# Two sorts of expert rows instead of three in a fused attention and mixture-of-experts block, and a weight ring of five places

## The reference, cut to what matters

```python
x = x + tanh(g_xattn[0]) * L0_xattn(layernorm(x), ctx)
x = x + tanh(g_ffn[0])   * L0_ffn(layernorm(x))      # 8 experts, top 2
x = x + tanh(g_xattn[1]) * L1_xattn(layernorm(x), ctx)
x = x + tanh(g_ffn[1])   * L1_ffn(layernorm(x))      # MLP 256-1024-1024-1024-256

# L0_ffn
probs = softmax(xf @ Wr);  topk_p, topk_i = top_k(probs, 2)
out = sum_k topk_p[k] * (xf @ Wi[topk_i[k]]) @ Wo[topk_i[k]]
# L1_ffn
h = silu(x @ w1 * s1) * (x @ w2 * s2)
h = gelu(h @ h1 * t1);  h = gelu(h @ h2 * t2);  return h @ w3 * s3
```

## Time and profile before

| | |
|---|---|
| median of 3 runs | 1046.01 us (1044.91 to 1046.17) |
| the profiled execution: time, span | 1046.19 us, 1044.4 us |
| granted TensorE clock, mean | 0.994 |
| busy: PE, DVE, ACT, POOL | 97%, 48%, 46%, 29% |
| sorted groups 2 and 4, period | 120.1 and 120.2 us |
| groups 1, 3, 5, 6, period | 91.7 to 91.8 us |

### The profile page before, as it was taken

One profiled execution on the slowest core, in us unless ns is written; L12 is line 12 of the kernel. 1 busy time (PEld: TensorE's weight loads), 2 busy tenths in 40 slices (PEclk: granted clock), 3 DMA queues, 4 the chain that ended last, 5 costly groups with the idle time before them and its releaser, 6 DMA issues.

```text
span 1044.4 us, 14384 instructions
## 1 busy us (share of the span) xinstructions
PE 1012.4 (97%) x5218; PEld 823.8 (79%) x5218; DVE 500.7 (48%) x1388; ACT 477.0 (46%) x877; POOL 303.4 (29%) x428
## 2 busy tenths in 40 slices
PE   7999999899999999999999999999999999999996
PEld 4778777678789877887898878778888788788885
DVE  5487768676343543463325434643245245134321
ACT  1355545446544545364344453644444435434431
POOL 0015653311710541216205423153044221112111
PEclk9999999999999999999999999999999999999999
DMA  9930015513475554344755553537545535344440
GB/s 340 378 121 1 2 61 168 187 52 102 141 259 182 178 155 151 115 146 132 251 177 157 178 155 98 160 121 252 187 152 191 161 102 180 103 135 147 141 141 23
DMA packets 44252, 158.85 MB, mean 152 GB/s; under 512 B 6443, under 2 KB 6827, under 8 KB 43282
## 3 DMA queue, kind: packets, MB, share of 16 engines
q0 software_dynamic: 29952, 104.88, 32.5%
q1 hardware_dynamic: 10826, 40.63, 11.4%
q10 hardware_dynamic: 3400, 12.38, 3.0%
HBM read 137.93 MB, written 29.36 MB: 160 GB/s over the span
## 4 chain that ended last, share of the span: by engine, by line
PE 83%; DVE 8%; ACT 4%; issue 2%; DMA 1%; POOL 1%; DVEq 0%; SPq 0%; POOLq 0%; ACTq 0%
PE psum L1027 56%; PE psum L921 2%; PE psum L1099 2%; PE psum L1101 2%; PE psum L1100 2%; PE psum L1075 1%; PE psum L820 1%; DVE x_residual L1882 1%; PE psum L830 1%; PE psum L678 1%; PE psum L947 1%; PE psum L702 1%; PE psum L716 1%; PE psum L929 1%; DVE ln_stats L1574 1%
## 5 line engine op out<-in xcount | busy, mean ns | idle before, releaser
L2258 POOL DMA_DIRECT2D mlp_pieces<-in_mlp x176 | 96.8, 557 | 424.2 <-PE psum L1027 420.7
L1027 PE MATMUL psum<-hidden_a_high,mlp_pieces 128*128 128x512 f32 x512 | 205.7, 402 | 0.0
L1027 PE MATMUL psum<-hidden_b_high,mlp_pieces 128*128 128x512 f32 x512 | 202.9, 396 | 0.0
L1027 PE MATMUL psum<-hidden_a_low,mlp_pieces 128*128 128x512 f32 x512 | 199.6, 390 | 0.0
L1027 PE MATMUL psum<-hidden_b_low,mlp_pieces 128*128 128x512 f32 x512 | 199.6, 390 | 0.0
L2105 DVE TENSOR_TENSOR hidden_a_low<-hidden_a,hidden_a_high 128x512 fp32r<-128x512 f32 x128 | 88.1, 688 | 174.2 <-ACT hidden_a_high L1497 173.4
L2105 DVE TENSOR_TENSOR hidden_b_low<-hidden_b,hidden_b_high 128x512 fp32r<-128x512 f32 x64 | 44.4, 693 | 169.6 <-ACT hidden_b_high L1497 169.6
L1027 PEld LDWEIGHTS psum<-hidden_a_high,mlp_pieces 128*128 128x128 f32 x512 | 96.1, 188 | 23.6 <-issue 2.8
L1514 ACT ACTIVATE hidden_a<-psum,mlp_scales 128x512 f32<-128x512 f32 x64 | 44.1, 689 | 154.4 <-PE psum L1027 154.4
L1027 PEld LDWEIGHTS psum<-hidden_a_low,mlp_pieces 128*128 128x128 f32 x512 | 96.2, 188 | 21.7 <-issue 2.6
L1027 PEld LDWEIGHTS psum<-hidden_b_high,mlp_pieces 128*128 128x128 f32 x512 | 96.2, 188 | 20.2 <-issue 0.8
(11 more groups left out here) (283 smaller groups left out, 1809.6 us busy)
## 6 DMA issues: line engine op xcount, KB each, us to landing
mlp_pieces<-in_mlp POOLq DMA_DIRECT2D x176, 512.0 KB, 4.0
slots<-in_zeros SPq DMA_DIRECT2D x3, 3072.0 KB, 36.6
yrows<-expert_rows ACTq DMA_DIRECT2D x18, 512.0 KB, 3.0
mlp_piece_to_examine<-in_mlp SPq DMA_DIRECT2D x16, 512.0 KB, 4.0
slot_rows<-slots SPq DMA_DIRECT2D x15, 512.0 KB, 4.5
x_residual<-in_x SPq DMA_DIRECT2D x4, 1024.0 KB, 24.2
out<-x_residual SPq DMA_DIRECT2D x8, 512.0 KB, 3.4
expert_in<-in_Wi SPq DMA_DIRECT2D x1, 2048.0 KB, 15.7
```

The costliest lines, as they stand in the source:

```text
L1027: last = mm(o, a, b, start=(k == 0 and i == 0), stop=(k == n_k - 1 and i == len(parts) - 1))
L2258: pool.dma_start(mlp_ring[:, r % RING, :], d["mlp"][r % NCHECK]).then_inc(ring_in[r % RING], 16)
```

## The change

Batches 2 and 3 are sorted together. `SORTS` has two entries, batch 1 alone and batches 2 and 3: 23 and 39 slot tiles (2 x 16 + 7), 62 in place of 69, in 12 and 20 pairs. Batch 1 stays where it was. The double sort is routed in group 1 (`ranked_in`), its expert products stand in group 2 (`routed_in`), and group 4 has neither. `xm` holds one batch, so the second batch is normalised over the first after the transposes of the first; its rows are scattered in group 1, and batch 2's rows are normalised once more in group 2 (`r_norm_again`) and scattered there. The ring has five places, which makes room for routing buffers of 16 tiles.

```diff
-RING = 6
+RING = 5
-NSB = B - 1
-EB = 23
+SORTS = [(1, 1), (2, 2)]
+EB = [2 * n + E - 1 for n in NJ]
...
+        def ranked_in(n):
+            return n if n < NS else None
+        def turns_at(s, w12, c):
+            if s == 0:
+                return c - 1 if w12 and 1 <= c <= 4 else None
+            return (c - 1 if 1 <= c <= 4 else None) if w12 else (c + 4 if c < 4 else None)
+        def logits_at(s, w12, c):
+            if s == 0:
+                return c - 2 if w12 and 2 <= c <= 5 else None
+            return (c - 2 if 2 <= c <= 5 else None) if w12 else (c + 3 if 1 <= c < 5 else None)
+        def steps_of(s):
+            if s == 0:
+                return {"copy": -2, "max": -1, "exp": 0, "mask": 0, "rank": 1, "coef": 1, "slots": 1, "tiles": 3}
+            return {"copy": 4, "max": 5, "exp": 5, "mask": 6, "rank": 6, "coef": 7, "slots": 7, "tiles": 10}
+        def pairs_at(s, c):
+            if s == 0:
+                return {3: (0, 1), 4: (2, 3, 4), 5: (5, 6), 6: (7, 8, 9), 7: (10, 11)}.get(c, ())
+            return {1: (0, 1, 2), 2: (3, 4, 5), 3: (6, 7, 8), 4: (9, 10, 11), 5: (12, 13, 14), 6: (15, 16, 17),
+                    7: (18, 19)}.get(c, ())
...
 PE, r_turn:
+                    bank = 6 + p % 2 if p < 4 else 4 + p % 2
+                    pe.wait_ge(xm_r, 2 * (R0[s] + p) + 2)
 PE, group, after the product of t:
+                            if r is not None and layer == 0 and turns_at(r, False, c) is not None:
+                                r_turn(r, turns_at(r, False, c))
+                            if r is not None and layer == 0 and logits_at(r, False, c) is not None:
+                                r_logits(r, logits_at(r, False, c))
+                            if r is not None and t == steps_of(r)["rank"]:
+                                r_rank(r)
 ACT, group, after gelu and high of t:
+                            if r is not None and layer == 0 and turns_at(r, False, c) is not None:
+                                r_turn(r, turns_at(r, False, c))
+                            if r is not None and HC * layer + c == steps_of(r)["exp"]:
+                                r_exp(r)
 DVE:
+            def r_norm_again(s):
+                dve.wait_ge(sc_done[s], 16 * 2 * JT)
+                for j in range(JT):
+                    normalise(JT + TJ[s] + j, xm[:, j, :], xa_r)
 DVE, group, w12, after the product with silu of c and low of c - 1:
+                        if r is None and c == 2 and s is not None and NJ[s] > JT:
+                            r_norm_again(s)
 DVE, group, after low of t:
+                            if r is not None and NJ[r] > JT and t < 4:
+                                r_norm(r, t + 4)
+                            if step.get("copy") == t:
+                                r_copy(r)
+                            if step.get("max") == t:
+                                r_max(r)
+                            if step.get("mask") == t:
+                                r_mask(r)
 POOL:
+                    if r == 1 and 14 <= piece < 22:
+                        if piece == 14:
+                            pool.wait_ge(ix_r, 2)
+                        scatter(1, (JT + piece - 14,))
+                    if n == 2 and 2 <= piece < 6:
+                        if piece == 2:
+                            pool.wait_ge(xa_r, JT)
+                        scatter(1, (2 * piece - 4, 2 * piece - 3))
```

More of the change, by code:

```diff
@@ L51 @@
 PIECE = 1024
-RING = 6
+RING = 5
 ND = 2
-NSB = B - 1
-EB = 23
-CHUNK = 4
-NCK = -(-EB // CHUNK)
-ROWS_B = NCK * CHUNK * P
-PAIRS = -(-EB // 2)
+SORTS = [(1, 1), (2, 2)]
+NS = len(SORTS)
+NJ = [n * JT for b, n in SORTS]
+TJ = [(b - 1) * JT for b, n in SORTS]
+EB = [2 * n + E - 1 for n in NJ]
+JM, EM = max(NJ), max(EB)
+CHUNK = 4
+NCK = [-(-n // CHUNK) for n in EB]
+PAIRS = [-(-n // 2) for n in EB]
+CK0 = [sum(NCK[:i]) for i in range(NS)]
+Q0 = [sum(PAIRS[:i]) for i in range(NS)]
+E0 = [sum(EB[:i]) for i in range(NS)]
+R0 = [sum(NJ[:i]) // 2 for i in range(NS)]
+assert all(n % 2 == 0 for n in NCK)
 XT0 = NT + G * ND
@@ L179, in program @@
[L179 to L194, removed]
+        rlg = place("weights", "batch_logits", [P, JM, 2 * E])
@@ L195, in program @@
+        cursor["weights"] = kept
+        kept = cursor["weights"]
+        row4 = place("weights", "slot_row", [P, JM, 2], at=rtop_at)
+        cursor["weights"] = kept
+        kept = cursor["weights"]
+        eq = place("weights", "is_slot", [P, JM, E], at=rpex_at)
+        cursor["weights"] = kept
         ti = place("weights", "count_integer", [P, E], I32)
@@ L402, in program @@
         eid_r = sem("tile_experts_ready")
-        sc_done = [sem(f"rows_scattered_{b}") for b in range(NSB)]
+        sc_done = [sem(f"rows_scattered_{b}") for b in range(NS)]
         xs_in = [sem(f"slot_rows_loaded_{h}") for h in range(2)]
@@ L565, in _ @@
                 load_x(b)
[L566 to L568 removed]
+            for i in range(NS):
+                dst = slots[i].rearrange("(c p j) d -> p c (j d)", c=NCK[i], j=CHUNK)
+                sp.dma_start(dst, d["zeros"].unsqueeze(1).broadcast_to([P, NCK[i], CHUNK * D])).then_inc(fill_done, 16)
             sp.wait_ge(r2_ps, 2 * B)
@@ L1132, in group @@
                         last.then_inc(d1_ps, 1)
[L1133 to L1136, removed]
+                        if r is not None and turns_at(r, True, c) is not None:
+                            r_turn(r, turns_at(r, True, c))
+                        if r is not None and logits_at(r, True, c) is not None:
+                            r_logits(r, logits_at(r, True, c))
                     for layer, (name, src) in enumerate((("h1", ha), ("h2", hb))):
@@ L1506, in group @@
                             high(c - 1, ha_f, ha_h, h_r, HC * n + c)
-                        if s is not None and 1 <= c <= 4:
-                            r_turn(s, c - 1)
+                        if r is not None and turns_at(r, True, c) is not None:
+                            r_turn(r, turns_at(r, True, c))
                     high(HC - 1, ha_f, ha_h, h_r, HC * n + HC)
@@ L2308, in _ @@
                         invert(G * (n + 2), G, STATS_A + n + 3)
-                    r = NCHECK * n + piece + RING
-                    if r < NCHECK * NG:
-                        load_piece(r)
-                if s is not None:
-                    for h in range(2):
-                        pool.wait_ge(st_done[h], 16 * NCK // 2 * (s + 1))
+                    p = NCHECK * n + piece + RING
+                    if p < NCHECK * NG:
+                        load_piece(p)
+                if gathers_after(n):
+                    if s is not None:
+                        for h in range(2):
+                            pool.wait_ge(st_done[h], stores_of(h, s))
+                    else:
+                        pool.wait_ge(cb_r, G * n)
                     gather(n + 2)
@@ L2390 @@
     for n in ("slots", "yrows"):
-        d[n] = [nc.dram_tensor(f"{n}_{b}", (ROWS_B, D), F32, kind="Internal").ap() for b in range(NSB)]
+        d[n] = [nc.dram_tensor(f"{n}_{b}", (NCK[b] * CHUNK * P, D), F32, kind="Internal").ap() for b in range(NS)]
     program(nc, d)
```

365 lines of the change are left out of this document (214 added, 151 removed).

## The result

The changed kernel takes 1063.39 us (median of 4 runs, 1061.94 to 1064.91) against 1045.53 us for the kernel before beside it: a ratio of 1.0162, interval 1.0147 to 1.0176. The forecast was 1063.2, slower with a chance of 0.91.

The account below looks back on a forecast made before the run. The prediction took PE, busy for 97% of the span, to bound the kernel. Its terms, -8.6 + 11.9 + 5.2 + 2.7 + 9.0 - 3.0 = +17.2 us, gave 1063.2 us, range 1052 to 1070.

Parts of the forecast that it names:

- What bounds the kernel: Whole kernel: PE is busy for 97% of the span, so only what PE waits for counts, and in full.
- Savings: Groups 1 to 4: seven tiles fewer -6.5, ranks made twice -0.5, waits gone -1.6; together -8.6 us.
- Transposes in group 1: Group 1, t = 0 to 3: PE waits for the second batch's normalised rows, 2.98 us four times, +11.9.
- Ranks: Group 1, t = 6: PE waits for the mask, made late by the exponential and table reload, +5.2 us.
- Second normalisation: Group 2, w12: DVE waits for group 1's scatters, then normalises again, and PE's product 5 waits, +2.7 us.
- Clock: After the six long waits of groups 1 and 2 PE's clock drops, 1.5 us each, +9.0 us; bounds 0 and 10.2.
- The rival without the clock: Groups 1 and 2: the waits are there but the clock stays up, 1054.2 us; chance 0.14.
- Before stage_d: Before 208 us: scores come 1.3 us earlier, PE's wait shrinks to 0.4 and no slow stretch follows, -3.0 us.
- Ring of five: Starts of groups 3 and 5: loads issued one piece earlier still land in time, 1.4 us early; cost 0, bounds 0 and 5.
- The sum: Whole kernel: all terms together +17.2 us, giving 1063.2 us against the median.

Follow-up runs that it names:

- all_three: The changed kernel with the edits of norm_early, rank_late and again_late together: 1033.85 us, ratio 0.9879 to the kernel before.
- exp_late: The changed kernel with only the second batch pair's exponential moved on ScalarE from step 5 to 6, behind the gelu: 1061.18 us, ratio 1.0144.
- norm_early: The changed kernel with each normalisation of the second batch in group 1 issued one step earlier on VectorE: 1044.90 us, ratio 0.9992.
- rank_late: The changed kernel with PE's rank products of group 1 moved from behind product 6 to behind product 7: 1054.85 us, ratio 1.0070.
- fill: The changed kernel with unread extra PE products ahead of the waits in groups 1 and 2, those of group 2 misplaced behind the wait: 1057.61 us, ratio 1.0101.
- fill_mended: As fill, against the changed kernel, but group 2's extra products (13) stand ahead of PE's wait in w12: 1052.92 us, ratio 1.0070.
- ring5_before: The kernel before with five places in the ring in place of six, nothing else: 1044.35 us, ratio 0.9985.
- again_late: The changed kernel with group 2's second normalisation moved behind w12 and the last eight tiles' scatters to pieces 5 to 8: 1058.29 us, ratio 1.0114.

## Why the prediction was right, point by point

**What bounds the kernel.** Right: PE's waits count in full. Four waits of 2.81 removed took away 11.2 us and the clock that went with them; of the other waits only the one in w12 moved, by 0.5.

**Savings, -8.6.** Not measured by themselves, but bounded by all_three: between the adds of groups 0 and 2 it takes 232.28 - 211.90 = 20.4 us more than the kernel before, and it saves 28.5 in group 4. That is -8.1, with a wait of 0.4 left in it that the forecast didn't have. Sized within 0.5, if the three edits left nothing else behind.

**Transposes in group 1, 2.98 each.** Measured 2.81 four times. DVE's timeline of the changed kernel at t = 0 has the chain as it was worked out:

```profile
369.53 0.69 DVE L2227 TENSOR_TENSOR hidden_b_low<-hidden_b,hidden_b_high 128x512 fp32r<-128x512 f32 x1 [2.21 <-ACT hidden_b_high L1594]
370.14 0.73 DVE L1684 TENSOR_SCALAR x_norm_of_batch<-x_residual,ln_mean_var,ln_rstd 128x256 f32<-128x256 f32 x2
```

The normalisations end at 370.87 and PE starts at 370.93. PE's product had ended at 370.93 - 2.81 = 368.12, ACT's gelu starts at 368.15 and `low` 1.38 later, as in the earlier trace rows. The forecast's 2.98 and the profile's 2.81 don't count from the same point: the forecast counts from the start that the next matmul would have had, and matmuls start 0.23 apart but last 0.39, so that this point lies some 0.17 before the modelled end of the last one. The last matmul here started at 367.71; from 367.94 to 370.93 it is 2.99. The term was sized rightly.

**Ranks, 5.2.** Measured 5.22, and by exp_late in the two parts of the forecast: 3.65 for the chain (forecast 3.6) and 1.57 for the late gelu (1.6). ACT's timeline of the changed kernel:

```profile
411.36 1.28 ACT L1564 ACT_TABLE_LOAD   x1
413.53 0.31 ACT L1564 ACTIVATE batch_exp<-batch_logits_less_max 128x128 f32<-128x128 f32 x1 [0.88 <-DVE batch_logits_less_max L2118]
413.75 1.07 ACT L1485 ACTIVATE x_norm_c_T<-psum 128x512 f32<-128x512 f32 x2
414.83 1.28 ACT L1611 ACT_TABLE_LOAD   x1
416.13 0.69 ACT L1611 ACTIVATE hidden_b<-psum,mlp_scales 128x512 f32<-128x512 f32 x1
```

The first load of a table lies in the time in which ACT waits for DVE; only the second stands in the chain. The rule of the Trainium skill ("ScalarE: Activation LUTs", What ACT_TABLE_LOAD costs), by which each switch drains for some 1.38 us more and the wait would have been about 7.1, is not borne out: the copies end at 414.82, the load starts at 414.83 and the gelu 0.02 after its end. The row decided rightly.

**Second normalisation, 2.7.** Measured 3.5; 3.0 or 3.1 in the executions of the four variants that left it in place (norm_early, rank_late, exp_late, fill). The eight normalisations took 2.67, as put (a third each). The last scatter had landed 3.38 us after its start where 2.43 had been taken. That is the term, and it was 0.3 to 0.8 too small.

**Clock, 9.0.** The place of the largest doubt, and fill_mended gives 10.4, just over the upper bound of 10.2. Of the six waits five were followed by a low stretch in the profiled execution; the first, at 370.93, was not. Some lost more than the 1.7 taken for each: 388 to 394 us, behind the third, lost 0.48 x 6 = 2.9 (the 3.4 in the expectation of norm_early takes in 386 to 388, when PE mostly stood). Five stretches of 2.1 on average stand where the forecast had six of 1.5; that the products are close is luck. The forecast's remark that waits of 0.40 and 0.59 left the clock at 1.00 in w12 was read from a row that ends at 459.20, before the wait of 0.59 at 467.32; the clock of the kernel before is 1.00 there too. The rival without the clock, 1054.2, is refuted as a forecast; as a number it is close to what fill_mended took, 1052.92.

**Before stage_d, -3.0.** In the profiled execution -3.25 and a wait of 0.41, as put; but the ring alone brings 1.9 between the medians, and 340.76 - 338.44 = 2.3 between the profiled executions. Both of these traces have lost the stretch behind the scores and kept the one at 148 us; the wait of 0.82 is 0.4 of what is missing. In the changed kernel ACT gets the first piece of the ring at 205.19, in ring5_before at 205.78. Why wasn't tried; the two clearing transfers, which the forecast put at nothing, are one of the differences. Besides, a low stretch of some 1.8 us comes and goes between executions, so that a single profile can't size this term.

**Ring of five, 0.** Right as to the time: no matmul waits for `mlp_pieces` in any of the traces. But the spare time was put too high, at 1.4 us. In fill_mended a weight load (`PEld`) of the second hidden product of group 3 waits 0.41 us for its piece, at 613.10, 5.0 after the first load behind the gathers goes out at 608.10; one in group 5 waits 0.18. In the changed kernel the same two points, 619.25 and 624.14, are 4.9 apart. The ring of five is at its edge where the forecast said it would be tightest.

**The sum.** Terms forecast for groups 1 to 4: -8.6 + 11.9 + 5.2 + 2.7 + 9.0 = +20.2; measured 50.37 - 28.50 - 0.03 = +21.8. With -3.25 at the start that is +18.6, and the end of the program gives 2.9 back, which no step had named: +15.7 in the profiled pair, +17.9 between the medians. The split between the groups was a little off: group 1 took 130.92 us where near 128 was forecast, group 2 131.35 for near 132. The forecast of +17.2 is right in its mechanism and in its terms; that it came within 0.2 us of the median is also luck, since 1.6 too little in the groups stands against the unnamed 2.9 at the end.

**Open.** Why 7.6 us follow the issue of the last output transfer in both kernels of the old layout (with rings of six and five) and 4.6 to 5.4 in all eight of the new one, wasn't tried. Its part in the medians isn't known either.

## What to carry to other kernels

When one engine is full, an operation that another engine makes for it should stand in that engine's program a whole product before the place where it is wanted (in norm_early one product was enough): with both at the same step, the full chain of the step (here gelu, split, normalise) shows up as idle time each time, and it can be summed beforehand from four rows of the old trace. The clock behind such waits has to be added: here 10.4 us on 20.0 us of waits. Where a merger of two stages makes a kernel slower, look first at the offsets of the merged steps: three edits here turned +1.6% into -1.2%.

## What the runs showed of the hardware

- The granted clock doesn't follow the length of a wait alone. A wait of 2.81 us at 370.93, one of 3.65 in exp_late and one of 3.05 in fill (windows above) were followed by 1.00, while three of the same 2.81 in the changed kernel and one of 3.0 in norm_early were followed by 0.65 or less. The windows behind the last one, of norm_early:

```profile
466.00:468.00 2.00, 1.41 (x4) 0.77 0.90 326
468.00:470.00 2.00, 2.00 (x6) 0.50 0.28 100
```

- The same wait in the same place can end either way. PE's wait of 1.15 us at 148 to 151 us stands in all ten traces, and a window of 2 us at 0.50 to 0.55 follows it in seven; in norm_early, fill_mended and all_three the clock stays at 1.00. Behind the first of the four waits of 2.81 it stays at 1.00 in the changed kernel and in again_late, and falls below 0.6 in rank_late and exp_late; behind the fourth it is the other way round.

- Products whose result nobody reads, put into time in which TensorE would have waited, made the kernel 10 us faster (1063.39 to 1052.92), with no useful work moved.
- Between executions of one kernel the time spreads by 4.6 us (norm_early, 1042.37 to 1046.92, 10 runs), 5.9 (the kernel before, 1042.86 to 1048.75, 17 runs) and 8.2 (exp_late, 4 runs, the slowest with the lowest mean clock). Low stretches in the part before 340 us come and go: in windows of 20 us the clock was 0.91 at 20 to 40 and 140 to 160 in rank_late, at 140 to 180 in again_late, and nowhere in norm_early, each 0.09 x 20 = 1.8 us.
